# Sixteen of a Mamba layer's 64 scan steps moved into an earlier attention stage, with scaling shifted to GpSimd and ScalarE

## The reference

```python
# Mamba, per direction: 256 channels, 16 states, A = -exp(A_log)
def step(h, inp):
    xt, dlt, bt, ct = inp
    h = jnp.exp(dlt[:, :, None] * A) * h + (dlt * xt)[:, :, None] * bt[:, None, :]
    return (h, jnp.einsum('bdn,bn->bd', h, ct))
_, ys = lax.scan(step, h0, xs)
y = ys.transpose(1, 0, 2) + Dp * xc
# relative-bias attention, per head
scores = jnp.einsum('bhqd,bhkd->bhqk', q, k) + position_bias
attn = jax.nn.softmax(scores, axis=-1)
out = jnp.einsum('bhqk,bhkd->bhqd', attn, v)
# every layernorm
(x - m) / jnp.sqrt(v + eps)
```

## Time and profile before

| | us |
|---|---|
| median of 3 runs | 5552.94 |
| lowest and highest | 5540.51, 5564.2 |
| the profiled execution, its own time | 5545.3 |
| its span in the profile | 5543.6 |
| first sequence's `attn1` | 360 to 491 |
| first sequence's `heads` with a scan beside it | 507 to 763 |

### The profile page before, as it was taken

The page is one execution under the profiler, slowest core; times in us unless marked ns, Lnnn a source line. Parts: engine busy times, 40 slices in busy tenths (PEclk is TensorE's granted clock), DMA queues, the critical chain, the costliest instruction groups (busy, mean ns, idle before and its releaser), DMA issues. The chain is left out here.

```text
span 5543.6 us, 69676 instructions
## 1 busy us (share of the span) xinstructions
PE 4726.4 (85%) x22038; PEld 2207.0 (40%) x22038; DVE 3555.6 (64%) x8259; ACT 2738.1 (49%) x5070; POOL 1481.6 (27%) x1876
## 2 busy tenths in 40 slices
PE   4689887988879888898878988789887998989888
PEld 2134344443444324443244433444334543444344
DVE  5766856678556785667755587656865568456545
ACT  2255553555526554365542755435644455436453
POOL 2712620136101461105501064010730117200200
PEclk8889998999989999899989999999988999999789
DMA  3411310123101231012210132001320113101000
GB/s 130 146 35 60 115 62 1 47 67 107 53 3 54 73 110 35 3 54 92 91 34 4 53 113 84 20 23 45 119 74 13 35 50 118 67 2 54 1 27 6
DMA packets 150524, 315.98 MB, mean 57 GB/s; under 512 B 16208, under 2 KB 24912, under 8 KB 150112
## 3 DMA queue, kind: packets, MB, share of 16 engines
q1 hardware_dynamic: 150128, 311.17, 17.4%
HBM read 307.89 MB, written 3.21 MB: 56 GB/s over the span
## 5 line engine op out<-in xcount | busy, mean ns | idle before, releaser
L196 PE MATMUL BANKS<-WB 128*128 128x512 bf16 x1616 | 454.3, 433 | 194.1 <-DVE XN L440 56.5
L758 POOL TENSOR_TENSOR heads_work<-heads_work,heads_c_all 128x512 f32<-128x512 f32 x384 | 487.2, 1271 | 380.5 <-DVE heads_work L792 367.9
L1503 ACT ACTIVATE heads_prob<-BANKS 128x512 f32<-128x512 f32 (+3 forms) x768 | 377.3, 518 | 289.4 <-PE BANKS L1398 283.5
L212 POOL TENSOR_TENSOR rstd<-rstd,WF 128x4 f32<-128x4 f32 x24 | 24.2, 1007 | 1665.9 <-DVE rstd L230 1665.9
L725 PE MATMUL BANKS<-heads_work,WF 128*128 128x512 f32 x768 | 444.2, 664 | 0.4
L196 PEld LDWEIGHTS BANKS<-WB 128*128 128x128 bf16 x1616 | 166.7, 108 | 443.0 <-issue 216.7
L1398 PE MATMUL BANKS<-heads_parts_kT,heads_parts_qT 64*128 64x512 bf16 (+3 forms) x768 | 240.5, 363 | 69.3 <-DVE heads_nmax L1544 46.9
L405 POOL TENSOR_TENSOR rstd<-rstd,WF 128x4 f32<-128x4 f32 x48 | 48.5, 1010 | 936.7 <-DVE rstd L426 935.9
L2143 ACT COPY attn_probt<-BANKS 128x512 f32<-128x512 f32 x384 | 223.9, 583 | 126.1 <-PE BANKS L2069 123.7
L2164 DVE CUSTOM_DVE_ANT_0 attn_biased<-BANKS,attn_toep 128x512 f32<-128x512 f32 x384 | 263.1, 685 | 33.5 <-DMA attn_toep<-bias_line 20.4
L1541 DVE CUSTOM_DVE_ANT_0 BANKS<-BANKS,WF 128x384 f32<-128x384 f32 (+3 forms) x512 | 243.1, 503 | 64.0 <-PE BANKS L1398 60.9
(11 more groups left out here) (891 smaller groups left out, 10594.6 us busy)
## 6 DMA issues: line engine op xcount, KB each, us to landing
heads_c_all<-bc_rows SPq DMA_DIRECT2D x384, 256.0 KB, 3.2
heads_b_all<-bc_rows SPq DMA_DIRECT2D x192, 256.0 KB, 3.5
attn_toep<-bias_line SPq DMA_DIRECT2D x96, 448.0 KB, 4.3
last_x_w<-in_w SPq DMA_DIRECT2D x48, 512.0 KB, 3.6
s_c_all<-bc_rows SPq DMA_DIRECT2D x64, 256.0 KB, 3.3
yheads_c_all<-bc_rows SPq DMA_DIRECT2D x64, 256.0 KB, 3.2
s_b_all<-bc_rows SPq DMA_DIRECT2D x32, 256.0 KB, 3.6
yheads_b_all<-bc_rows SPq DMA_DIRECT2D x32, 256.0 KB, 3.5
```

Of the source, the lines that this page charges most:

```text
L196: nc.tensor.matmul(bank, ident_b, bc(ident_b[:, 0:1], [P, SEQ]), start=True, stop=True)
L758: nc.gpsimd.tensor_tensor(work[:, m % RW, :], work[:, m % RW, :], c_all[:, m % RC, :], ALU.mult).then_inc(rd, 1)
L1503: nc.scalar.activation(prob[:, i % PR, lo:hi], bank("T", i)[:, lo:hi], ACT.Exp).then_inc(exped, 1)
```

## The change

A new piece, `mamba_early`, runs the first 16 steps (forward direction, first channel tile) of the next sequence's scan beside `attn1`. It uses no TensorE: both rows come by DMA, GpSimd makes drive, product and running sum, ScalarE the decay into bank 6, VectorE the scan. `mamba_scan` gets `first=16` and does the other 48 beside `heads`, with a planned step of 4.52. The attention of `attn1` becomes `attn1_parts`, planned at 2.05 a unit: GpSimd scales all 64 units (`scale_by_act` is (0,)), VectorE copies every fourth transposed tile and ScalarE the others, the projection of each pair goes through `RING` and is added into `X` by VectorE, and the transposes come five units behind the scores instead of four. In `heads` the norms subtract on VectorE without waiting for the power, and ScalarE scales. The first rotary layer's memsets move behind the norm. The loop gets `hint_back_edge=True`.

```diff
@@ norm_parts
+            if scaled_by_act:
+                for j in range(NJ):
+                    last = V.tensor_scalar(dst[:, j, :], src[:, j, :], s_mv[:, j, 0:1], None, ALU.subtract)
+                last.then_inc(centred, 1)
+            else:
+                yield at + 3.2
+                dve.wait_ge(rooted, 1)
+            for j in range(0 if scaled_by_act else NJ):
...
         def scalar(act):
+            if scaled_by_act:
+                yield at + 3.2
+                act.wait_ge(centred, 1)
+                act.wait_ge(rooted, 1)
+                for j in range(NJ):
+                    nc.scalar.activation(dst[:, j, :], dst[:, j, :], ACT.Copy, scale=s_rstd[:, j:j + 1]).then_inc(normed, 1)
@@ mamba_scan
-    def mamba_scan(st, dest, START, STEP):
-        STEPS = 2 * ND * NS
+    def mamba_scan(st, dest, START, STEP, first=0):
+        STEPS = 2 * ND * NS - first
+        BEGUN = first // NS
@@ new
+    def mamba_early(st, K, START, STEP):
+        work = st.sb("e_work", [P, 2, SEQ])
+        b_rows = XNM[:, :, :].rearrange(line), XTM[:, :]
+        c_rows = XO[:, :, :].rearrange(line), XN[:, :, :].rearrange(line)
+        total = XM[:, :, :].rearrange(line)
+        DECAY = PS[6]
...
+            def fetch_b(m):
+                if m >= 2:
+                    sp.wait_ge(driven, m - 1)
+                sp.dma_start(b_rows[m % 2], row(0, m)).then_inc(b_ld[m % 2], 16)
+            def fetch_c(m):
+                if m >= 2:
+                    sp.wait_ge(multiplied, m - 1)
+                sp.dma_start(c_rows[m % 2], row(1, m)).then_inc(c_ld[m % 2], 16)
...
+                yield at(m) - 0.6 * STEP
+                if m:
+                    act.wait_ge(scanned, m)
+                nc.scalar.activation(DECAY, delta[:, 0, m // NS, :], ACT.Exp, scale=W("A")[:, a:a + 1]).then_inc(decayed, 1)
...
+            def drive(m):
+                pool.wait_ge(b_ld[m % 2], 16 * (m // 2 + 1))
+                if m >= 2:
+                    pool.wait_ge(added, sums(m - 1))
+                    pool.wait_ge(multiplied, m - 1)
+                nc.gpsimd.tensor_tensor(work[:, m % 2, :], b_rows[m % 2], du[:, 0, m // NS, :], ALU.mult).then_inc(driven, 1)
+            for m in range(-2, K):
+                if m >= 0:
+                    yield at(m) + 0.3 * STEP
+                    pool.wait_ge(scanned, m + 1)
+                    pool.wait_ge(c_ld[m % 2], 16 * (m // 2 + 1))
+                    nc.gpsimd.tensor_tensor(work[:, m % 2, :] if n else total, work[:, m % 2, :], c_rows[m % 2],
+                                            ALU.mult).then_inc(multiplied, 1)
+                    if n:
+                        yield at(m) + 0.5 * STEP
+                        nc.gpsimd.tensor_tensor(total, total, work[:, m % 2, :], ALU.add).then_inc(added, 1)
+                if m + 2 < K:
+                    yield at(m + 2) - 1.2 * STEP
+                    drive(m + 2)
...
+                yield at(m) - 0.2 * STEP
+                dve.wait_ge(driven, m + 1)
+                dve.wait_ge(decayed, m + 1)
+                V.tensor_tensor_scan(work[:, m % 2, :], DECAY, work[:, m % 2, :], 0.0, ALU.mult, ALU.add).then_inc(scanned, 1)
+                if m % NS == NS - 1:
+                    V.scalar_tensor_tensor(ysum[:, t, :], xc[:, 0, t, :], W("D")[:, t:t + 1], total,
+                                           ALU.mult, ALU.add).then_inc(flushed, 1)
@@ new, in the place of the attention written out in attn1
+    def attn1_parts(st, scale_by_act, copy_by_act):
+        EXP, SCALE, TURN = 2, 3, 5
+        NS_, NP_, NT_ = 4, 6, 2 * PAIR
+        RING = (PS[4], PS[7])
+        def at(s):
+            return 2.05 * s
...
+        def gpsimd(pool):
+            for e in range(U):
+                if not scaled_by_act(e):
+                    yield at(e + EXP) + 1.6
+                    pool.wait_ge(inverted, e + 1)
+                    nc.gpsimd.tensor_scalar(prob[:, e % NP_, :], prob[:, e % NP_, :], rden[:, e:e + 1], None,
+                                            ALU.mult).then_inc(scaled_p, 1)
...
+            def add(p):
+                V.tensor_tensor(X[:, :, :], X[:, :, :], RING[n % 2].rearrange(tiles, j=NJ), ALU.add).then_inc(summed, 1)
...
+                if 0 <= u < U and not copied_by_act(u):
+                    yield at(s) + 1.4
+                    V.tensor_copy(probt[:, u % NT_, :], RING[n % 2]).then_inc(copied_v, 1)
@@ memsets of the first rotary layer
-                yield at - 5.0
+                yield at
+                pool.wait_ge(ready, 2)
@@ both_attentions
-                            spare=WEIGH, idle=10)
+                            spare=WEIGH, idle=10, scaled_by_act=True)
@@ layers and the loop
-            streams = [mamba_scan(st, XM, 4.0, 3.4)] if scan_next else []
+            streams = [mamba_scan(st, XM, 4.0, 4.52, EARLY)] if scan_next else []
+    EARLY = 16
+            streams = [mamba_early(st, EARLY, 13.5, 7.97)] if scan_next else []
+            streams.append(attn1_parts(st, (0,), (1, 1, 1, 0)))
-    with nc.Fori(0, n - 2) as b:
+    with nc.Fori(0, n - 2, hint_back_edge=True) as b:
```

More of the change, by code:

```diff
@@ L394, in norm_parts @@
     def norm_parts(st, tag, src, dst, small, at, dst_t=None, banks=None, rms=False, sq=None, gain_t=None, gain=None,
-                   shift=None, after=None, spare=None, idle=0, later=()):
+                   shift=None, after=None, spare=None, idle=0, later=(), scaled_by_act=False):
         s_stats, s_mv, s_rstd = small
@@ L682, in decay, with step @@
             return PS[2] if m % 2 else (XNM[:, :, :].rearrange("p j d -> p (j d)"), XTM[:, :])[m // 2 % 2]
-        def step(i):
+        def step(m):
+            i = first + m
             return i // (ND * NS), i // NS % ND, i % NS
@@ L719, in tensor @@
                 if m >= 0:
-                    n = m % NS
+                    n = step(m)[2]
                     yield at(s) + 0.45 * STEP
+                    if m == 0 and n:
+                        nc.tensor.matmul(SUM, ident, XM[:, :, :].rearrange("p j d -> p (j d)"), start=True, stop=False)
                     pe.wait_ge(rd, m + 1)
                     if n == 0 and m:
-                        pe.wait_ge(emptied, m // NS)
+                        pe.wait_ge(emptied, (first + m) // NS - BEGUN)
                     nc.tensor.matmul(SUM, ident, work[:, m % RW, :], start=(n == 0), stop=(n == NS - 1)).then_inc(acc, 1)
@@ L783, in vector @@
                     V.tensor_tensor(DRIVE, DRIVE, du[:, d, t, :], ALU.mult).then_inc(drv[0], 1)
-                if s >= NS and n == LATE:
+                if first + s >= NS * (BEGUN + 1) and n == LATE:
                     yield at(s) + 0.2 * STEP
-                    flush(s // NS - 1)
+                    flush((first + s) // NS - 1)
                 yield at(s) + 0.5 * STEP
@@ L1992, in layers @@
-            weighed, emptied, projected = (st.sem(n) for n in ("weighed", "emptied", "projected"))
-            def unit(u):
-                return u // PAIR, u % PAIR // 2, u % 2
-            def made_in(s):
-                i = MAKE_AT.get(s % PAIR)
-                if i is None or s >= U:
-                    return None
-                r = s // PAIR + (i < 2)
-                return (r, i) if r < NPAIR else None
-            place = {("make", 0, 0): 0, ("make", 0, 1): 1}
-            for s in range(LAST):
-                if 0 <= s - TURN < U:
-                    place["turn", s - TURN] = len(place)
-                if made_in(s):
-                    place[("make",) + made_in(s)] = len(place)
```

465 lines of the change are left out of this document (286 added, 179 removed).

## The result

The changed kernel takes 5629.0 us (median of 4 runs, 5616.9 to 5633.6), the kernel before 5554.8 beside it: a ratio of 1.0128, 95% interval 1.0102 to 1.0154. It is 1.3% slower. The forecast was 5408, 2.6% faster, with a range of 5360 to 5475. The profiled execution has a span of 5631.9 us, 88.3 more than before.

The account below looks back on a forecast made before the run. TensorE was taken to bound `attn1`, with VectorE and TensorE sharing the bound in `heads`. 5545.3 - 129.5 + 22 - 16 - 16 = 5405.8 us for the profiled execution, plus 2 for the median: 5408, range 5360 to 5475.

Parts of the forecast that it names:

- Part 2: `attn1`: 16 scan steps enter in seven stages, 3 us each, plus 1 us in the last sample's; +22 us.
- Rival (a): `attn1`: GpSimd becomes the bound if a scaling costs 1.27 us; stage grows 10 to 13 us, kernel 5467; chance 0.15.
- Rival (b): `attn1`: GpSimd and VectorE hold each other up, GpSimd operations at 1.769 us; +65 us a stage, kernel 5842; chance 0.05.
- Part 1: `heads`: 16 scan steps leave in seven stages, each 18.5 us shorter; -129.5 us.
- Part 3: `heads`, eight stages: norms scaled by ScalarE and memsets moved win 2 us each, second norm 0; -16 us.
- Part 4: Loop's branch: the hint shortens the wait at five taken branches, at most 18 us; taken as -16 us.
- (d): `attn1`: banks stall TensorE through late copies behind scans and the projection in the ring; +19 us a stage, 5520; chance 0.06.

Follow-up runs that it names:

- e4: The changed kernel with GpSimd's scaling written as a product of two tensors, the second a spread column; 5379.6 us (one time).
- e16: The changed kernel with only the copies of transposed probabilities moved, all to ScalarE; 5584.1 us (one time).
- e11: The changed kernel with GpSimd's scaling as a product with a spread column and all copies on ScalarE; 5359.2 us, 0.9678 of the kernel before.
- e8: The changed kernel with VectorE scaling in `attn1` and ScalarE making all copies; 5360.3 us, 0.9676 of the kernel before.
- e15: e8 with VectorE's scaling written as a product with a spread column; 5411.4 us, 0.9779 of the kernel before.
- e3: The changed kernel with no scan steps in `attn1`, all 64 in `heads`; 5479.3 us, 0.9895 of the kernel before.
- e12: e8 with 24 scan steps in `attn1` instead of 16; 5408.1 us, 0.9759 of the kernel before.
- e10: The changed kernel with VectorE scaling the two norms of `heads` again, memsets left where the change put them; 5637.4 us.

## Why the prediction was wrong

**Part 2 is the step that failed, in its price of GpSimd's scaling.** It read "one input and a scalar a row is nearer to the copy: I take 0.65". The runs show 1.572, above both bounds that I had set. Its sum of GpSimd's work, 101 us, was 156 to 158. With that, its path fell too: TensorE did not end the stage, its transposes waited for GpSimd. The stage grew by 41.3 us where I charged 3. The form carries 31.3 of these: e4 changes nothing else and brings `attn1` from 181.0 to 149.7. The banks carry 3.6 as the kernel stands (e16) and 6.5 once the form is mended (e4 to e11). What is left, 143.2 against 139.7, is the size of my +3; what it is made of, no run separates. The copy was the wrong neighbour because I chose by the count of inputs; the nearest in operation was a product. The trace had no row of GpSimd with a scalar a row, and two rows of other forms held no bound for it.

**Rival (a) named the mechanism**, GpSimd as the bound, at 1.27. Rival (b) had the place where it turns into a loss: a load of about 154 us, at +23 a stage. The load came to 156 to 158 and the stage to +41, because I had let GpSimd's work fill the whole stage. It can't: it begins behind the first row of B (idle 6.8 us before its first drive) and is followed by the last units' transposes, weighting and projection; GpSimd is busy 158.1 us of 180.3. (b)'s own reason, the two engines slowing each other, wasn't at work: the products kept 1.28.

Rival (b) drew on the page "GPSIMD Engine Reference" of the Trainium skill. Its rule did show itself in e8 and e15, where VectorE got the scaling: 0.486 became up to 1.55, and 0.693 up to 1.82. The Trainium skill's page "SBUF — State Buffer" (section "Who interferes with whom") says that VectorE's `tensor_scalar`, where it runs in a two-port mode, and a `tensor_tensor` with both inputs in SBUF contend with GpSimd; the two runs agree in that both forms were held up. In which mode the first one ran, no trace shows.

**Part 1 was right.** 16 steps less took 245.9 - 227.3 = 18.6 us off a stage (e3 to the changed kernel), 19.5 in e8; I had 18.5. Part of so close a match is luck: the clock in these stages went from 0.955 to 0.937 on the way, which the estimate did not have. Seven stages: -130. That the last steps cost more than the mean one did not carry on: the next eight gave nothing (e12), with the granted clock down.

**Part 3 was mis-sized.** I took 2 us a stage and nothing for the second norm. With 64 steps the two edits are worth 9.2, of which 4.1 lie behind the second norm, at a clock that rose with them; with 48 steps the scaling alone is worth 1.9, which is 3.2 won behind the second norm and 1.4 lost ahead of it. I had read 4.85 us for four scalings against memsets, but not that over both norms the median was 1.278: the second norm collides as a rule, and the subtraction, which I expected to collide too, doesn't, as it is done beside the power. By the way over e3, 9.2 of the 27.8 us that `heads` lost are Part 3's and 18.6 Part 1's; with the steps taken away first, Part 3's share is smaller (e10), so the two don't simply add.

**Part 4 failed.** I took 16 us for five edges, nearly all of the 18 that I expected VectorE's wait to lose. That wait did fall, from 7.5 to 4.6 us, but the edges got only 10 us shorter, of which the run without the hint leaves 3 to it. TensorE's own branch, the one that counts, still takes 2.8 us in the median, 4.1 in the run without the hint and 3.5 before. What VectorE wins at the branch is mostly lost behind it: `last` shrank by 5.0 us and `moe0` grew by 3.0. That it is lost waiting for TensorE, I read from the branch's time. The rule that I cited from the Trainium skill's page "Runtime: NRT & Kernel Launch" makes such a branch a fetch of code, and speaks of no hint; I had assumed that a hint hides all of it, and the rows say that it doesn't.

In the chances, "most of (d)" doesn't fit the sum: 0.91 holds 0.02 of its 0.06.

Against the forecast of 5405.8 for the profiled execution: Part 2 cost 270 more (292 for 22), Parts 1 and 3 together won 50 more (195.2 for 145.5), Part 4 and the rest won 7 less (8.9 for 16). 5405.8 + 270.4 - 49.7 + 7.1 = 5633.6, the time of the profiled execution. The version that beats both kernels by these findings is the changed one with the product form and all copies on ScalarE (e11), or with VectorE's scaling and all copies on ScalarE (e8): 3.2% below the kernel before.

## What to carry to other kernels

An operation that the trace doesn't show on an engine has no price until one run measures that very form; here two spellings of one multiplication differ by 0.53 us, and 64 of them a stage decide the sign. Add up the load of the engine that receives the work, stage by stage, with the time at both ends of the stage in which it can't work, and ask at which load it turns. Behind the first bound look for the second: a bank of a short ring that is emptied from the queue of a busy engine held the stage up as soon as the first was gone.

## What the runs showed of the hardware

- GpSimd's multiplication of a 128x512 tile by one value a row: 1.572 us with the scalar from memory, 1.489 with a constant, 1.040 as a product with a spread column. A product of two full tiles is 1.27, a copy 0.614.
- VectorE's 128x512 scaling beside GpSimd's products: 0.486 undisturbed, median 0.696 and up to 1.55 disturbed; as a product 0.693, median 0.961 and up to 1.82, and GpSimd's sums are then at 1.60 for 1.34, its drives at 1.55 for 1.29. Its scans (1.21) and its reductions out of a bank (0.68) kept their time in every run.
- A stage with less work had the lower granted clock: TensorE in the first `heads` was granted 0.95 with 48 scan steps and 0.90 with 40, and was busy 195.5 us for 193.6 with fewer instructions. What brought the clock down was not tested.
